# Three rings of attention buffers, from whole tiles to blocks

## The reference

```
x = x + LN(attn(LN(x)))          # 16 heads of 64, causal, with biases
x = x + LN(ffn(LN(x)))           # 8 experts: select, gate, low-rank update
scores = q k^T / sqrt(64); scores[k > q] = -inf
probs  = softmax(scores);  attn = probs v;  out = attn wo^T + bo
```

## Time and profile before

| | |
|---|---|
| median of 3 runs | 2557.71 us (2556.71 to 2563.8) |
| profiled execution | 2565.57 us, of which the span is 2563.6 us |
| TensorE busy | 2326.1 us |
| ACT, DVE, POOL busy | 1782.1, 1734.0, 1713.2 us |
| granted TensorE clock, mean | 0.965 |

### The profile page before, as it was taken

One profiled execution on the slowest core, in us unless ns is written; L12 is line 12 of the kernel. 1 busy time (PEld: TensorE's weight loads), 2 busy tenths in 40 slices (PEclk: granted clock), 3 DMA queues, 4 the chain that ended last, 5 costly groups with the idle time before them and its releaser, 6 DMA issues. The chain is left out here.

```text
span 2563.6 us, 72165 instructions
## 1 busy us (share of the span) xinstructions
PE 2326.1 (91%) x28626; PEld 1453.4 (57%) x28626; DVE 1734.0 (68%) x4154; ACT 1782.1 (70%) x2579; POOL 1713.2 (67%) x1519
## 2 busy tenths in 40 slices
PE   4999999999999998889999999999997559999995
PEld 2566656565757655556675757575664334544542
DVE  8577867776767755456676666666666545777776
ACT  3477877777777766567777787777787745666665
POOL 4587878888878876668888888888887741222221
PEclk9999999999999999999999999999998669999997
DMA  9699999999999999989999999999999975666663
GB/s 240 131 188 184 203 182 194 194 188 183 205 183 194 180 190 189 189 154 178 176 184 173 182 182 171 189 169 180 171 162 202 169 161 121 156 160 160 162 165 83
DMA packets 1433647, 450.18 MB, mean 176 GB/s; under 512 B 1410240, under 2 KB 1411536, under 8 KB 1433312
## 3 DMA queue, kind: packets, MB, share of 16 engines
q1 hardware_dynamic: 1433312, 445.57, 94.9%
HBM read 67.95 MB, written 41.94 MB: 43 GB/s over the span
## 5 line engine op out<-in xcount | busy, mean ns | idle before, releaser
L815 POOL TENSOR_TENSOR hl<-probs,hl 128x1024 f16<-128x1024 f32 (+7 forms) x768 | 1231.3, 1614 | 404.5 <-ACT hl L696 402.8
L690 ACT ACTIVATE probs<-s_ps,exp_bias 128x1024 f32<-128x1024 f32 (+7 forms) x768 | 655.1, 853 | 415.4 <-DVE exp_bias L541 411.0
L538 DVE TENSOR_REDUCE neg_max<-s_ps 128x1 f32<-128x1024 f32 (+7 forms) x768 | 694.9, 905 | 69.4 <-PE s_ps L396 69.1
L696 ACT ACTIVATE hl<-probs 128x1024 f16<-128x1024 f32 (+7 forms) x768 | 620.5, 808 | 50.4 <-DMA pt<-hl 26.4
L414 PE MATMUL o_ps<-v,pt 128*128 128x65 f16 x4352 | 454.0, 194 | 86.3 <-DMA pt<-hl 75.4
L396 PE MATMUL s_ps<-nat 64*128 64x512 f16 (+3 forms) x3840 | 438.0, 357 | 68.4 <-ACT probs L690 65.3
L414 PEld LDWEIGHTS o_ps<-v,pt 128*128 128x128 f16 x4352 | 404.4, 97 | 140.2 <-DMA pt<-hl 65.9
L415 PE MATMUL o_ps<-v,pt 128*128 128x65 f16 x4352 | 453.8, 195 | 0.0
L416 PE MATMUL o_ps<-v,pt 128*128 128x65 f16 x4352 | 451.8, 193 | 0.0
L443 PE MATMUL u_ps<-arena,w 128*128 128x512 f16 x1008 | 391.5, 388 | 39.7 <-DMA arena<-hl 34.9
L415 PEld LDWEIGHTS o_ps<-v,pt 128*128 128x128 f16 x4352 | 404.3, 98 | 26.6 <-issue 0.3
(11 more groups left out here) (150 smaller groups left out, 3686.4 us busy)
## 6 DMA issues: line engine op xcount, KB each, us to landing
w_raw<-in_w_pairs SPq DMA_DIRECT2D x48, 576.0 KB, 4.8
o_scratch<-o_hl SPq DMA_DIRECT2D x128, 128.0 KB, 2.4
out<-result SPq DMA_DIRECT2D x32, 512.0 KB, 2.9
x_in<-in_x SPq DMA_DIRECT2D x27, 512.0 KB, 4.9
pt<-hl SPq DMA_TRANSPOSE x768, 4.6
nat<-in_x SPq DMA_DIRECT2D x16, 512.0 KB, 4.5
xn_scratch<-xn SPq DMA_DIRECT2D x16, 512.0 KB, 4.6
xn<-in_x SPq DMA_DIRECT2D x11, 512.0 KB, 3.7
```

The costliest lines, as they stand in the source:

```text
L538: nc.vector.tensor_reduce(neg_max[:, r, acc, h:h + 1], s_ps[n % S_RING][:, 0:nb * P], AX_X, ALU.max, negate=True).then_inc(max_done, 1)
L690: nc.scalar.activation(probs[n % P_RING][:, 0:nb * P], s_ps[n % S_RING][:, 0:nb * P], ACT.Exp, bias=exp_bias[:, r, acc, h:h + 1], scale=SO ...
L696: nc.scalar.activation(hl[n % HL_RING][:, 0:nb * P], probs[n % P_RING][:, 0:nb * P], ACT.Copy).then_inc(p_hi_done, 1)
L815: nc.gpsimd.tensor_tensor(hl[n % HL_RING][:, w:2 * w], probs[n % P_RING][:, 0:w], hi, ALU.subtract).then_inc(p_lo_done, 1)
```

## The change

`probs`, `hl` and `pt` each become one buffer of 24, 40 and 40 blocks (`hl` and `pt` have two halves per block). A task takes as many blocks as it has, behind the task before; where they don't fit before the end it starts at 0 again. A function lists for every task the earlier tasks whose blocks it overwrites, and the waits are for those. The landing of a transpose is told by one of 16 semaphores instead of 4, and a transpose doesn't start before task n - 16 is multiplied. In bytes for each partition, `probs` stays at 12 KB, `hl` goes from 24 KB to 20 KB and `pt` from 16 KB to 20 KB.

```diff
-S_RING, P_RING, HL_RING, PT_RING = 3, 3, 6, 4
+S_RING = 3
+P_BLOCKS, HL_BLOCKS, PT_BLOCKS, T_RING = 24, 40, 40, 16
+TASK_BLOCKS = [nb for p in range(PAIRS) for t, k0, nb, acc in steps_of(p) for h in range(2)]
+def ring(capacity):
+    at, before, live, pos = [], [], [], 0
+    for n, nb in enumerate(TASK_BLOCKS):
+        pos = 0 if pos + nb > capacity else pos
+        before.append([m for m in live if at[m] < pos + nb and pos < at[m] + TASK_BLOCKS[m]])
+        live = [m for m in live if m not in before[n]] + [n]
+        at.append(pos)
+        pos += nb
+    return at, before
+P_AT, P_BEFORE = ring(P_BLOCKS)
+HL_AT, HL_BEFORE = ring(HL_BLOCKS)
+PT_AT, PT_BEFORE = ring(PT_BLOCKS)
...
-                    if n >= PT_RING:
-                        sp.wait_ge(pv_done, n - PT_RING + 1)
+                    read = max([n - T_RING] + PT_BEFORE[n]) + 1
+                    if read >= 1:
+                        sp.wait_ge(pv_done, read)
                     sp.wait_ge(p_lo_done, n + 1)
-                    sp.dma_start_transpose(pt[n % PT_RING][:, 0:2 * nb, :], hl[n % HL_RING][:, 0:2 * nb * P]).then_inc(
-                        pt_done[n % PT_RING], 16)
+                    sp.dma_start_transpose(pt_of(n), hl_of(n, 2)).then_inc(pt_done[n % T_RING], 16)
...
-                if n >= P_RING:
-                    act.wait_ge(p_lo_done, n - P_RING + 1)
+                if P_BEFORE[n]:
+                    act.wait_ge(p_lo_done, max(P_BEFORE[n]) + 1)
...
-                if n >= HL_RING:
-                    old = n - HL_RING
-                    act.wait_ge(pt_done[old % PT_RING], 16 * (old // PT_RING + 1))
+                for old in HL_BEFORE[n]:
+                    act.wait_ge(pt_done[old % T_RING], 16 * (old // T_RING + 1))
```

More of the change, by code:

```diff
@@ L142, in attend_phase @@
         v = [sb(f"v{i}", [P, QT, 2, 2, HD + 2], F16) for i in range(2)]
-        probs = [sb(f"probs{i}", [P, CHUNK * P], F32) for i in range(P_RING)]
-        hl = [sb(f"hl{i}", [P, 2 * CHUNK * P], F16) for i in range(HL_RING)]
-        pt = [sb(f"pt{i}", [P, 2 * CHUNK, P], F16) for i in range(PT_RING)]
+        probs = sb("probs", [P, P_BLOCKS * P], F32)
+        hl = sb("hl", [P, 2 * HL_BLOCKS * P], F16)
+        pt = sb("pt", [P, 2 * PT_BLOCKS, P], F16)
         neg_max = sb("neg_max", [P, N_ROUND, 3, 2], F32)
@@ L204, in attend_phase @@
         p_lo_done = sem("p_lo_done")
-        pt_done = [sem(f"pt_done{i}") for i in range(PT_RING)]
+        pt_done = [sem(f"pt_done{i}") for i in range(T_RING)]
         pv_done = sem("pv_done")
@@ L270, in dst_of, with probs_of, hl_of, pt_of @@
             return nat[p % 2][:, 2 * WHICH[m] + part, c * 512:(c + 1) * 512]
+        def probs_of(n):
+            return probs[:, P_AT[n] * P:(P_AT[n] + TASK_BLOCKS[n]) * P]
+        def hl_of(n, part):
+            first, nb = 2 * HL_AT[n], TASK_BLOCKS[n]
+            return hl[:, (first + (nb if part == 1 else 0)) * P:(first + (nb if part == 0 else 2 * nb)) * P]
+        def pt_of(n):
+            return pt[:, 2 * PT_AT[n]:2 * (PT_AT[n] + TASK_BLOCKS[n]), :]
+        def first_hl(i):
+            return hl[:, i % 4 * 2 * D:(i % 4 + 1) * 2 * D]
         def shaped(m, tile):
@@ L293, in transpose_probs @@
             def transpose_probs(p, i):
-                nb = steps_of(p)[i][2]
                 for h in range(2):
                     n = NTASK * p + 2 * i + h
-                    if n >= PT_RING:
-                        sp.wait_ge(pv_done, n - PT_RING + 1)
+                    read = max([n - T_RING] + PT_BEFORE[n]) + 1
+                    if read >= 1:
+                        sp.wait_ge(pv_done, read)
                     sp.wait_ge(p_lo_done, n + 1)
-                    sp.dma_start_transpose(pt[n % PT_RING][:, 0:2 * nb, :], hl[n % HL_RING][:, 0:2 * nb * P]).then_inc(
-                        pt_done[n % PT_RING], 16)
+                    sp.dma_start_transpose(pt_of(n), hl_of(n, 2)).then_inc(pt_done[n % T_RING], 16)
             def store_rows(p, half):
@@ L369, in _ @@
                     load_x(x_first[i % X_RING], x_loaded[i % X_RING], 0, i + X_RING)
-                transpose_x(i, i, hl[i % 4][:])
+                transpose_x(i, i, first_hl(i))
                 after = {"k": "v", "v": "q"}.get(FIRST_SPLITS.get(i))
@@ L405, in times_v @@
                     pe.wait_ge(unit_lo_done, units_before(p, [("v", c) for c in range((k0 + nb + 3) // 4)]))
-                pe.wait_ge(pt_done[n % PT_RING], 16 * (n // PT_RING + 1))
+                pe.wait_ge(pt_done[n % T_RING], 16 * (n // T_RING + 1))
                 if first and done >= 1:
@@ L410, in times_v @@
                 for k in range(nb):
-                    hi, lo = pt[n % PT_RING][:, k, :], pt[n % PT_RING][:, nb + k, :]
+                    hi, lo = pt_of(n)[:, k, :], pt_of(n)[:, nb + k, :]
                     v_hi, v_lo = (v[p % 2][:, k0 + k, part, h, 0:HD + 1] for part in range(2))
@@ L644, in _ @@
                     norm_stats(i + 1, x_first[(i + 1) % X_RING], x_loaded[(i + 1) % X_RING], (i + 1) // X_RING)
-                xn_low(i, x_first[i % X_RING], hl[i % 4])
+                xn_low(i, x_first[i % X_RING], first_hl(i))
                 if i in FIRST_SPLITS:
@@ L687, in exponentials @@
                 act.wait_ge(bias_done, n + 1)
-                if n >= P_RING:
-                    act.wait_ge(p_lo_done, n - P_RING + 1)
-                nc.scalar.activation(probs[n % P_RING][:, 0:nb * P], s_ps[n % S_RING][:, 0:nb * P], ACT.Exp,
+                if P_BEFORE[n]:
+                    act.wait_ge(p_lo_done, max(P_BEFORE[n]) + 1)
+                nc.scalar.activation(probs_of(n), s_ps[n % S_RING][:, 0:nb * P], ACT.Exp,
                                      bias=exp_bias[:, r, acc, h:h + 1], scale=SOFTMAX_SCALE).then_inc(exp_done, 1)
                 act.wait_ge(exp_done, n + 1)
-                if n >= HL_RING:
-                    old = n - HL_RING
-                    act.wait_ge(pt_done[old % PT_RING], 16 * (old // PT_RING + 1))
-                nc.scalar.activation(hl[n % HL_RING][:, 0:nb * P], probs[n % P_RING][:, 0:nb * P], ACT.Copy).then_inc(
-                    p_hi_done, 1)
+                for old in HL_BEFORE[n]:
+                    act.wait_ge(pt_done[old % T_RING], 16 * (old // T_RING + 1))
+                nc.scalar.activation(hl_of(n, 0), probs_of(n), ACT.Copy).then_inc(p_hi_done, 1)
             def chunk_factors(p, r):
@@ L779, in _ @@
                     act.wait_ge(xt_done[i % 4], 16 * (i // 4))
-                xn_high(i, x_first[i % X_RING], hl[i % 4])
+                xn_high(i, x_first[i % X_RING], first_hl(i))
                 if i in FIRST_SPLITS:
@@ L811, in probs_low @@
             def probs_low(p, i, h):
-                n, w = NTASK * p + 2 * i + h, steps_of(p)[i][2] * P
+                n = NTASK * p + 2 * i + h
                 pool.wait_ge(p_hi_done, n + 1)
-                hi = hl[n % HL_RING][:, 0:w]
-                nc.gpsimd.tensor_tensor(hl[n % HL_RING][:, w:2 * w], probs[n % P_RING][:, 0:w], hi,
-                                        ALU.subtract).then_inc(p_lo_done, 1)
+                nc.gpsimd.tensor_tensor(hl_of(n, 1), probs_of(n), hl_of(n, 0), ALU.subtract).then_inc(p_lo_done, 1)
             def unit_low(p, u):
```

## The result

The changed kernel takes 2525.15 us (median of 4 runs, 2519.42 to 2525.55) against 2560.76 us (4 runs, 2556.71 to 2566.6) before: a ratio of 0.9861, with a 95% interval of 0.9847 to 0.9876. That is 36 us or 1.4%, where 14 us were forecast. The time lies in the stated range (2512 to 2567 us) and the direction is right.

A forecast was written before the change was run, and what follows sets the result against it. TensorE, busy 91%, was taken to set the pace, with SP's serial issue nearly as full. Terms 23 - 3 - 7 - 2 + 3 = 14 us gave a 2544 us median; range 2512 to 2567 us.

The forecast's parts named there:

- The step that failed: Starting bound: TensorE sets the attention phase's pace, so a buffer can win only its idle time, 237 us.
- (g): TensorE's granted clock: two falls to half clock behind waits for transposes saved, +3 us (0 to +10).
- (c): SP's transpose issues: closing pauses makes issues longer, giving back a third of the 23 us, -7 us.
- (b): TensorE's scores: 14% of the saved stall time turns into waits for exponentials, -3 us.
- The reading of SP's queue: SP's 35.9 us wait row in pair 5 disbelieved: 4.6 us idle counted, SP issuing for 92% of the time.
- (a): Transposed ring: slot waits move from n-4 mostly to n-6 or n-7, cutting TensorE's waits for transposes, 23 us gain.
- (d): Ring of pairs: ACT's copy waits for landings, tighter at each pair's second step, -2 us (-12 to +5).
- (e): Ring of probabilities: exponentials wait for POOL's task n-4, n-3 or n-2; nothing, with -12 us as bound.
- (f): Waits as instructions: 594 instead of 765 ahead of exponentials, about as many elsewhere; nothing.
- Nothing moves: Rival: SP and the DMA engines bind, earlier transposes lengthen the next; 0 to 7 us gained, chance 0.28.
- slower: Rival: ACT's copy at each pair's head waits for n-4 landings, giving 2572 us; chance 0.14.
- all stalls go: Rival: issue isn't elastic and head starts add up, saving 50 us, to 2508 us; chance 0.14.

The follow-up runs named there:

- half transposed kernels: Changed kernel and kernel before, each transposing only the high half of the probabilities, used also for the low: 2459.05 us (0.96) and 2460.37 us (0.9608).
- second profile of the changed kernel: The changed kernel run once more, unedited, in a later job: 2529.17 us, 0.9865 to the kernel before.
- runs by head: Changed kernel with the n-4 slot wait back for one head's transpose of each step: first head 2563.5 us (0.9995), second head 2537.26 us (0.9887).

## Why the prediction was right or wrong

**The step that failed** stands at the start: that a buffer can win only what TensorE idles. The whole worth beyond idle time was put into term (g), two falls of the clock, +3 us, and it measured 12.5 us. The second failure is (c), -7 us for longer issues, where nothing was given back. Of the 25.8 us that the forecast lacks against the 39.8 us of the profiled spans, 9.5 are (g)'s and 7 are (c)'s. Another 8 are (b)'s, which had waits for exponentials rise by 3 us where they fell by 5, within what two profiles differ by. The mechanism, a longer lead for the transposes, was right.

**The reading of SP's queue** was right. Its row of waits overstates the slot waits, SP is issuing for nine tenths of the time, and the half transposed kernels show that a transpose is late only under that pressure. Counted again, SP's idle time in front of transposes up to the last pair is 98 us and not 84, which changes no term. 90 us of it end when a slot comes free; in the changed kernel 2 us do. That part of (a) was right, and so was that POOL's low half comes next.

**(a)** is right in total and near in each stretch: 23 us forecast, 24.6 measured (10.4, 2.5, 9.3 and 2.4 against 11, 4, 6 and 2). 1133 to 1958 was taken too low: only 0.5 us is left there. The turn was taken too high, so the near match of the total is in part luck; against the second profile of the changed kernel (54.8) it is 20.6.

**(b)** -3 us: no such exchange. The waits for exponentials are 60.3 and 64.1 us in two profiles, 65.3 before.

**(c)** -7 us failed. That issues stretch with the load is shown by the half transposed kernels. But I took a share off a gain that I had already cut to 60% for SP's full queue, which counts one thing twice. Nothing was given back: the median issue is 1.867 us, and 1.888 in the second profile, where I expected 1.95, and 4.5 us to landing (4.6) where I expected 5. All issues of transposes in pairs 0 to 14 together take 1511 us before and 1482 and 1506 after.

**(d)** -2 us: nothing. ACT's waits for landings don't gather at the second step of a pair either; its two tasks have 4.4 of the 24.1 us. **(e)** nothing, and **(f)** nothing, as forecast; exponentials wait 2.5 us for POOL.

**(g)** +3 us is the term most mis-sized: TensorE's busy time fell by 12.5 us. The sign I gave came true, four falls of the clock up to 840 us where there were six up to 857, and was worth the 3 us; the rest lies elsewhere. In pairs 0 to 14 the stretches at 0.50 add up to 44.4 us before and 30.7 us after, and half of the difference is 6.8 us; the start phase has one fall more. That leaves 5 us or so that the clock doesn't explain: pair 9, which has no fall of the clock in either trace, went from 115.6 to 115.0 us. Why TensorE is busy for less there no run shows. The size of the term is rough, too: in nine profiles of kernels with a slot wait of n-5 or more TensorE is busy for 2305.8 to 2317.5 us, in three with n-4 for 2324.3 to 2326.1.

In the profiled executions: 24.6 + 5.0 + 12.5 = 42.1 us, less 2.3 us that came back in small waits elsewhere, most of them in the start phase, is the span's 39.8. The forecast had 23, -3 and 3 for the same, and -9 (terms (c) and (d)) for what didn't exist. Set against the run with the slot wait put back (72.3 to 50.7, 70.1 to 60.3, 2325.5 to 2313.6) the parts are the same within 5 us.

**Why one task of lead is enough** was not in the prediction. A step takes 115.9 / 24 = 4.8 us, and a transpose 4.6 us from issue to landing. From the end of task n-4's products to TensorE's use of task n there are 9.2 us at the median, for either head. Of these 4.6 go to the landing, so 4.6 us are left for what SP has to issue ahead of it, and a load and a few stores between long transposes use that up. What n-5 gives differs by head. For the first head, task n-5 ends a step earlier than n-4, a median of 4.6 us, since the scores and the unit of a step lie between the two; for the second head only its own products lie between them, and it is 0.6 us. And SP, which issues in order, stood for slots in front of the first head's transposes alone: 90 us in 82 places in the kernel before, none in front of the second's. That is what the runs by head confirm. TensorE's own waits would mislead here: 57.6 of the 75 us are for the second head's transposes, which come behind the first's.

That a further task brings nothing is measured, and the trace of the changed kernel shows why. SP stands 80 us in front of transposes up to the last pair, 70 of them until POOL's low half is there and 2 for a slot (64, 54 and 1 us in its second profile). With 44 blocks of `pt` it is 60, 50 and 2. The slot no longer ends any wait that counts; POOL's low half does.

**The rivals.** "Nothing moves" is refuted, "slower" too: the tight waits at `hl` exist and cost nothing. The time, 2525 us, fell into the bracket of "all stalls go" (2505 to 2532), which had a chance of 0.14. But that rival has the number for another reason: it took 50 us, 44 of them from stalls and 6 from the clock, where the stalls gave 24.6. It is right for the seven pairs from 1110 on and wrong for the turn and the last pair.

## What to carry to other kernels

A ring's depth is to be set against one step's length and the latency from issue to landing, in tasks of lead; here n-4 was just short and n-5 enough, and everything beyond was unused, since the producer ahead of the ring (POOL) was next. Ask for which task of a step the wait binds: the one that goes first. The bytes can come from giving each task the blocks that it has. When a wait of the engine that sets the pace goes, count the busy time that goes with it, here 12.5 us to 29.6, and don't discount one full queue twice.

## What the runs showed of the hardware

Idle time on TensorE cost more than its length: 68 us more of it brought 35 us more of busy time, with stretches of 3.4 us at half clock that begin 0.1 to 1.3 us behind the stalls. SP was held for some 1.2 us by issuing a DMA transpose of one to eight blocks when the queue had room (half the data), and for 1.87 us at the median, 2.36 for eight blocks, when it was full. And a row of waits of SP's queue can be nearly all illusion, as here 35.9 us for 4.6.
